# Making the convolution kernels inside the channel stage, and handing the last channel's rows over in SBUF

## The reference

```
x = x + mask * (causal_conv(x * mask, K) + D * x)   # K[h, l] = 2 Re sum_n Cs[h,n] exp(dtA[h,n] * l)
x = x + A1[id1] @ (B1[id1] @ x)                     # 8 adapters of rank 16
x = x + A2[id2] @ (B2[id2] @ x)                     # 64 adapters of rank 16
x = x + W[id3]^T x + bias[id3]                      # 32 matrices 64 x 64
```

## Time and profile before

| | |
|---|---|
| median of three runs | 784.39 us |
| the profiled execution | 783.29 us |
| its span, first to last instruction | 781.5 us |
| setup stage | 0 to 76 us |
| channel stage | 76 to 500 us |
| pair stage | 502 to 781.5 us |
| PE busy | 708.0 us (91%) |
| DVE busy | 624.3 us (80%) |
| ACT busy | 331.2 us (42%) |
| POOL busy | 393.9 us (50%) |
| granted clock of TensorE, mean | 0.989 |
| moved by DMA | 219.95 MB, mean 281 GB/s |

### The profile page before, as it was taken

The page is one execution under the profiler, slowest core; times in us unless marked ns, Lnnn a source line. Parts: engine busy times, 40 slices in busy tenths (PEclk is TensorE's granted clock), DMA queues, the critical chain, the costliest instruction groups (busy, mean ns, idle before and its releaser), DMA issues.

```text
span 781.5 us, 19175 instructions
## 1 busy us (share of the span) xinstructions
PE 708.0 (91%) x6688; PEld 541.4 (69%) x6688; DVE 624.3 (80%) x1124; ACT 331.2 (42%) x432; POOL 393.9 (50%) x682
## 2 busy tenths in 40 slices
PE   3044899999999999999999999589999999999997
PEld 2044677778887788887777777367777777777774
DVE  7995888887887778777877777378888888888885
ACT  2611112333133333222211122058777777777775
POOL 2420588888860000004767700177667766776672
PEclk9999999999999999999999999789999999999999
DMA  4007999999999999999999995579999999999974
GB/s 154 0 1 186 312 315 299 338 325 322 332 345 338 323 331 333 335 288 333 283 319 295 311 301 160 196 265 319 311 321 324 314 318 317 315 321 315 321 264 159
DMA packets 121319, 219.95 MB, mean 281 GB/s; under 512 B 19828, under 2 KB 79796, under 8 KB 121268
## 3 DMA queue, kind: packets, MB, share of 16 engines
q1 hardware_dynamic: 102692, 166.59, 66.3%
q10 hardware_dynamic: 9360, 33.56, 11.0%
q0 software_dynamic: 9216, 19.15, 7.7%
HBM read 146.35 MB, written 72.91 MB: 281 GB/s over the span
## 4 chain that ended last, share of the span: by engine, by line
PE 86%; DVE 3%; DMA 1%; ACT 1%; issue 0%; DVEq 0%; SPq 0%; ACTq 0%
PE ps L973 42%; PE ps L1261 11%; PE ps L1248 7%; PE ps L161 7%; PE ps L1294 6%; PE ps L1277 3%; PE ps L1276 3%; PE ps L1267 2%; PE ps L1034 1%; PE ps L1306 1%; PE ps L1018 1%; PE ps L1026 1%; DVE x1l L1235 1%; DMA xt<-x_rows 0%; DVE xTl L1216 0%; ACT xTh L1175 0%
## 5 line engine op out<-in xcount | busy, mean ns | idle before, releaser
L973 PE MATMUL ps<-toep,xTh 128*128 128x512 f16 (+3 forms) x1024 | 209.9, 300 | 0.0
L973 PE MATMUL ps<-toep,xTl 128*128 128x512 f16 (+3 forms) x512 | 147.0, 300 | 0.0
L783 POOL DMA_INDIRECT gnow<-g_rows,idx_g x64 | 58.8, 919 | 153.6 <-DMA g_rows<-g_out 127.4
L973 PEld LDWEIGHTS ps<-toep,xTh 128*128 128x128 f16 x1024 | 97.9, 98 | 51.1 <-issue 1.1
L1131 POOL DMA_INDIRECT asel<-a_rows,idx_a x64 | 72.2, 1129 | 77.3 <-PE ps L1277 76.2
L167 ACT ACTIVATE xS<-ps 128x256 f32<-128x256 f32 x64 | 24.4, 381 | 176.8 <-PE ps L161 176.8
L176 DVE TENSOR_TENSOR xTl<-ps,xTh 128x1024 f16<-128x1024 f32 x64 | 78.3, 1223 | 24.9 <-ACT xTh L168 24.6
L1126 POOL COPY bsel<-bt 128x256 f16 x256 | 92.7, 405 | 2.4 <-issue 1.7
L758 POOL DMA_INDIRECT wnow<-in_L_cond_weights,idx_w x64 | 62.1, 970 | 55.4 <-DVEq L920 38.4
L1216 DVE TENSOR_TENSOR xTl<-ps,xTh 128x1024 f16<-128x1024 f32 x64 | 78.3, 1224 | 12.3 <-ACT xTh L1175 9.0
L973 PE MATMUL ps<-diff,xTh 128*128 128x256 f16 x512 | 87.3, 273 | 0.0
(11 more groups left out here) (225 smaller groups left out, 1649.1 us busy)
## 6 DMA issues: line engine op xcount, KB each, us to landing
toep<-k_rows SPq DMA_DIRECT2D x64, 384.0 KB, 6.5
diff<-d_rows SPq DMA_DIRECT2D x64, 384.0 KB, 8.0
xt<-in_x SPq DMA_DIRECT2D x32, 512.0 KB, 6.3
x_rows<-xt ACTq DMA_DIRECT2D x32, 512.0 KB, 6.1
xt<-x_rows SPq DMA_DIRECT2D x32, 512.0 KB, 7.3
out_dram<-outt SPq DMA_DIRECT2D x32, 512.0 KB, 7.9
out_dram<-diff SPq DMA_DIRECT2D x32, 512.0 KB
toep<-x_rows SPq DMA_DIRECT2D x24, 512.0 KB
```

Of the source, the lines that this page charges most:

```text
L783: gp.indirect_dma_start(m.gnow[:, v, :], None, m.g_rows, bass.IndirectOffsetOnAxis(ap=m.idx_g[0:64, q:q + 1], axis=0)).then_inc(g_gathered ...
L973: last = PE.matmul(out, xs[x_part], rhs(part), start=start and k == 0, stop=stop and k == 2)
```

## The change

- K is made in eight chunks of eight channels. The setup stage makes chunk 0 only; chunks 1 to 7 are made in turns 0 to 6 of the channel stage, in pieces put into the lists of DVE, ACT, PE and SP at given channels u of a turn: the sines at u = 0 (ACT), combining at 1, the factors at 2 (both DVE), four products at 2 (PE), the first element at 3 (DVE), high and low parts at 4 (ACT, DVE), eight stores at 5 (SP, which then waits until they have landed), decays at 6 and 7 (ACT, sixteen small exponentials) and the turns of the chunk after at 6 and 7 (DVE).
- The sum's high part and the copy of the common part go from VectorE to ScalarE (`high_sum`, `copy_common`). `copy_common` of channel h-1 stands before the store of h-2 and waits for the convolution of h-1.
- The first seven channels of x are loaded in the setup stage. The rest of the setup (first adapters' turned A, bias, index rows) goes into the first turn of the channel stage (`finish_setup`).
- GpSimd waits for four gathers with one semaphore. Turns 5 and 6 are written out instead of a loop.
- For the first three pairs, channels 0 to 62 are loaded from DRAM as soon as these have landed, and the rows of channel 63 are copied from its SBUF tile; the DRAM copy of channel 63 is waited for only before the pairs from 3 on.

```diff
+E = 8
+CHUNKS = H // E
+KP = E // 2
+EARLY = 3
...
+def high_sum(nc, m, act, h, u):
+    act.wait_ge(m.xS_summed, h + 1)
+    nc.scalar.activation(m.xSh[:, u % 2, :, :], m.xS[:, u % 2, :, :], ACT.Copy).then_inc(m.xSh_ready, 1)
...
+def k_decay(nc, m, k, dst, s, ready):
+    for e in range(E):
+        nc.scalar.activation(dst[:, e, :], m.step[:, s, :], ACT.Exp, scale=m.par[:, 0, bass.ds(k * E + e, 1)]).then_inc(ready, 1)
...
+def k_products(nc, m, pe, k, bank):
+    pe.wait_ge(m.tables_ready, k + 1)
+    for q in range(KP):
+        last = nc.tensor.matmul(k_bank(m, bank)[:, q, :].rearrange("p (e c) -> p e c", e=2), m.u_all[:, 2 * q:2 * q + 2, :].rearrange("p e a -> p (e a)"),
+                                m.tv[:, q:E:KP, :], start=True, stop=True)
+    last.then_inc(m.k_done, 1)
...
+def store_k(m, sp, k):
+    sp.wait_ge(m.khl_ready, 2 * k + 2)
+    for e in range(2):
+        for n, rows in enumerate((m.k_rows, m.d_rows)):
+            for part in range(2):
+                dst = rows[bass.ds(k * E + e * KP, KP), part, 0:L].rearrange("q (a c) -> a q c", c=TC)
+                sp.dma_start(dst, m.khl[64 * e + 32 * n:64 * e + 32 * n + 32, part, :, :]).then_inc(m.k_stored, 16)
...
 (channel stage, SP)
+                            if make_k and u == XU - 3:
+                                store_k(m, sp, i + 1)
+                                sp.wait_ge(m.k_stored, 128 * (i + 2))
                             load_toeplitz(m, sp, h + 3, (u + 3) % U)
...
+                for p in range(EARLY):
+                    for b in range(2):
+                        sp.dma_start(x1_slot(m, p)[H * b:H * b + H - 1, :], m.x1_rows[2 * p + b, 0:H - 1, :]).then_inc(m.x1_parts[p], 16)
+                sp.wait_ge(low_ready, H)
+                sp.wait_ge(x1_ready, H)
+                for p in range(EARLY):
+                    sp.dma_start(x1_slot(m, p)[H - 1:P:H, :], x_slot(m, XU - 1)[2 * p:2 * p + 2, :]).then_inc(m.x1_parts[p], 16)
...
 (channel stage, ACT)
+                def copy_common(h, early):
+                    act.wait_ge(conv_done, h + 1)
+                    if not early:
+                        act.wait_ge(common_added, h)
+                    S.activation(m.common[:], conv_common, ACT.Copy).then_inc(common_copied, 1)
...
                             high_x(nc, m, u)
+                            high_sum(nc, m, act, h, u)
+                            copy_common(h - 1, first and u < 2)
                         if not (first and u < 2):
                             store_x1(h - 2, (u - 2) % XU)
+                        if make_k and u == 0:
+                            k_trig(nc, m, act, i + 1)
+                        if make_k and u == 4:
+                            act.wait_ge(m.k_stored, 128 * (i + 1))
+                            k_high(nc, m, act, i + 1, 3)
+                        if start_k and u == 6:
+                            act.wait_ge(m.tables_ready, i + 2)
+                            k_decay(nc, m, i + 2, m.dv, 0, m.decay_v_ready)
+                        if start_k and u == 7:
+                            k_decay(nc, m, i + 2, m.du, 1, m.decay_u_ready)
...
                 turns(act, body)
+                copy_common(H - 1, False)
                 store_x1(H - 2, XU - 2)
...
 (channel stage, DVE)
-                        dve.wait_ge(conv_done, h + 1)
-                        V.tensor_copy(m.common[:], conv_common).then_inc(common_added, 1)
-                        dve.wait_ge(common_added, 2 * h + 1)
+                        if make_k and u == 1:
+                            k_combine(nc, m, dve, i + 1)
+                        if make_k and u == 2:
+                            k_tables(nc, m, dve, i + 1)
+                        if make_k and u == 3:
+                            k_first(nc, m, dve, i + 1, 3)
+                        if make_k and u == 4:
+                            k_low(nc, m, dve, i + 1, 3)
+                        if start_k and u == 6:
+                            k_turns_u(nc, m, dve, i + 2)
+                        if start_k and u == 7:
+                            k_turns_v(nc, m, dve, i + 2)
+                        if first:
+                            finish_setup(u)
+                        dve.wait_ge(common_copied, h + 1)
```

More of the change, by code:

```diff
@@ L176, in low_x @@
     V.tensor_tensor(m.xTl[:, u % 2, :, :], m.turned, m.xTh[:, u % 2, :, :], ALU.subtract).then_inc(m.xTl_ready, 1)
[L177 to L183, removed]
+    dve.wait_ge(m.xS_summed, h + 1)
@@ new lines, in k_high, with k_low @@
+def k_high(nc, m, act, k, bank):
+    act.wait_ge(m.k0_added, k + 1)
+    for e in range(2):
+        rows = slice(64 * e, 64 * e + 64)
+        nc.scalar.activation(m.khl[rows, 0, :, :], k_bank(m, bank)[rows, :, e * TC:e * TC + TC], ACT.Copy).then_inc(m.k_high, 1)
+def k_low(nc, m, dve, k, bank):
+    dve.wait_ge(m.k_high, 2 * k + 2)
+    for e in range(2):
+        rows = slice(64 * e, 64 * e + 64)
+        nc.vector.tensor_tensor(m.khl[rows, 1, :, :], k_bank(m, bank)[rows, :, e * TC:e * TC + TC], m.khl[rows, 0, :, :],
+                                ALU.subtract).then_inc(m.khl_ready, 1)
@@ L317, in _ @@
+                sp.dma_start(m.biases[:], bias.rearrange("s o d -> s (o d)")).then_inc(m.bias_loaded, 16)
                 sp.wait_ge(const_made, 4)
-                sp.dma_start(m.k_rows[:, :, L:KPAD].rearrange("h s z -> (h s) z"), zeros[:]).then_inc(k_stored, 16)
+                sp.dma_start(m.k_rows[:, :, L:KPAD].rearrange("h s z -> (h s) z"), zeros[:]).then_inc(pad_stored, 16)
                 sp.dma_start(m.g_rows[GROW:GROW + R, :], ident[0:R, 0:R]).then_inc(m.g_stored, 16)
[L320 to L326, removed]
@@ L374, in _ @@
                              blocks(4).rearrange("p k t -> p t k"), ACT.Copy, scale=A_SCALE).then_inc(a_high, 1)
[L376 to L397, removed]
+                act.wait_ge(b_turned, 1)
+                S.activation(m.bt[:, 0:N1, 0, :, :], by_adapter(blocks(2)), ACT.Copy).then_inc(m.b0_high, 1)
+                k_high(nc, m, act, 0, 6)
+                high_sum(nc, m, act, 0, 0)
+                act.wait_ge(m.tables_ready, 1)
+                k_decay(nc, m, 1, m.dv, 0, m.decay_v_ready)
+                k_decay(nc, m, 1, m.du, 1, m.decay_u_ready)
+                act.wait_ge(m.decay_v_ready, 2 * E)
+                act.wait_ge(m.decay_u_ready, 2 * E)
+                act.wait_ge(m.b0_high, 1)
             @block.tensor
@@ L543, in _ @@
[L543 to L549 removed]
+                dve.wait_ge(m.par01_ready, 1)
@@ L684, in turns @@
         def turns(eng, body):
-            body(0, first=True)
+            body(0, first=True, make_k=True, start_k=True)
             with eng.Fori(1, GROUPED) as i:
-                body(i, group=True, next_group=True)
-            body(GROUPED, group=True)
-            with eng.Fori(GROUPED + 1, TURNS - 1) as i:
-                body(i)
+                body(i, group=True, next_group=True, make_k=True, start_k=True)
+            body(GROUPED, group=True, make_k=True, start_k=True)
+            for i in range(GROUPED + 1, TURNS - 1):
+                body(i, make_k=True, start_k=i < TURNS - 2)
             body(TURNS - 1, last=True)
@@ L698, in load_x, with body @@
                     sp.dma_start(x_slot(m, u), x[:, bass.ds(h, 1), :].rearrange("b o t -> b (o t)")).then_inc(m.x_loaded[u], 16)
-                def body(i, first=False, last=False, group=False, next_group=False):
-                    if first:
-                        for h in range(3, XU - 1):
-                            load_x(h, h)
+                def body(i, first=False, last=False, group=False, next_group=False, make_k=False, start_k=False):
                     for u in range(XU):
@@ L888, in selection_rows, with col, row_columns @@
+                pf, lf, rf, sf = (m.colf[:, n:n + 1] for n in range(4))
+                def col(n, rows=slice(0, P)):
+                    return cols[rows, n:n + 1]
+                pair = m.idf[:].rearrange("p n (q b) -> p n b q", b=2)
+                def row_columns():
                     step_of(V.tensor_scalar(col(3), lf, -1.0, 1.0, ALU.mult, ALU.add))
```

470 lines of the change are left out of this document (260 added, 210 removed).

## The result

The changed kernel took 796.71 us in the median of four runs (791.39 to 798.96) against 783.95 of the kernel before; the ratio is 1.0147, interval 1.0109 to 1.0186. The forecast was 778. The profiled execution has a span of 794.2 us against 781.5.

What follows compares the result with a forecast made beforehand. Setup, whatever delays TensorE's next channel (TensorE always busy, DMA 93%), and the hole before the pair stage count; 781.5-40.7+8.4+1.2+0.5+2.0+5.5+10+4+2.5 = 774.9 us span, so 778 us median, range 760 to 797.

Steps and rivals of the forecast that it cites:

- The setup: Before the channel stage: 256 instead of 2,048 elements a step, stage starting 39.5 us earlier; 40.7 less with channel 1's wait.
- K's products: TensorE, seven more chunks in the channel stage: 1.2 us each, 8.4 us in all, bounds 5.9 and 11.8.
- one full place: VectorE, channel 6 of the first turn: row numbers and K need 5.6 us against 3.6 of room, 2.0 us.
- I cost them at nothing: VectorE's pieces of K, 1.1 to 1.5 us, lie in some 1.65 us freed per channel by the moved copies.
- ScalarE's bursts: Sines and exponentials, 3.0 us each, 1.1 beyond the slack: 5.5 us in turns 0, 5 and 6; bounds 0 and 10.
- rival 3: ScalarE's table switches hold it about twice the load's length, five ungrouped ones 1.3 us more each: 784.5 us; chance 0.07.
- cover it: Grouped turns: a group's transposes or products on TensorE, 0.9 to 1.3 us behind the same channel, cover ScalarE's bursts.
- the late stores: Channel stores 5.2 us later delay loads of A in grouped turns: 10 us taken, bounds 0 and 19.4.
- mostly in the same microseconds in which TensorE is held up by A: Channel stage: K's stores on SyncE's queue, 20 us at full price, overlap the stalls for A, so 4 us taken.
- The argument for taking half: Late stores: a later TensorE leaves the DMAs less to carry, so part lands earlier; 10 us instead of 19.4.
- Rival 2: SyncE's queue bounds the grouped turns: late stores 19.4 and K's stores 20, 39.4 instead of 14; 803 us, chance 0.18.
- The hole: From last convolution to the pair stage's first transposes: 2.5 us longer, bounds 2 earlier and 5 later.

Runs made afterwards that it cites:

- Experiment 4: Changed kernel with ScalarE's store issued ahead of the sum's high part and common copy, and B and A loaded one channel earlier: 774.96 us, ratio 0.9861.
- experiment 2: Kernel before with one wait added: the store of channel h-2 is issued only when the convolution of h-1 is done; 797.93 us, ratio 1.0178.
- experiment 5: Changed kernel with K's eight stores of a turn issued from ScalarE's queue in channel 5 instead of SyncE's: 803.83 us, ratio 1.0255.

## Why the prediction was wrong

**The setup** was right: 39.5 us less forecast, 39.2 measured; the wait of 2.1 us at channel 1 went too.

**K's products** were over-sized, as the changed kernel's chain of waits shows (start, length, what):

```profile
184.57 1.34 PE ps L1149 x24
185.91 0.89 PE ps L311 x8
186.81 0.88 PE ps L190 x8
```

0.89 us a chunk, 6.2 in all against 8.4 forecast, near the lower bound of 5.9.

**VectorE** had one full place, as forecast. The transposes behind the index steps come 2.9 us late (2.0 forecast); TensorE's timeline in the changed kernel (start, length, engine, line, operation, idle before):

```profile
97.83 1.33 PE L190 MATMUL ps<-ident,xt 128*128 128x128 f32 x8 [2.89 <-DVE xSl L216]
```

But "I cost them at nothing" did not hold for its other pieces. In each of the four grouped turns TensorE waits, before it turns a group's B, for the low part of K that VectorE writes (us, times, longest):

```profile
PE ps L1116 <- DVE khl L336: 4.8, 4, 2.0
```

**ScalarE's bursts** had the right form. ScalarE's timeline in the third turn of the changed kernel:

```profile
222.90 1.28 ACT L265 ACT_TABLE_LOAD   x1 [0.28 <-issue]
224.20 0.42 ACT L265 ACTIVATE k_su<-k_tu 128x256 f32<-128x256 f32 x1
...
225.43 0.51 ACT L270 ACTIVATE k_tv<-k_tv,phase 128x256 f32<-128x256 f32 x1
```

3.0 us from the load to the last sine, as forecast, and the step behind the load starts at once, as in the earlier trace rows; rival 3 is out. From the transposes at 357.56 to the end at 502.47, 23 convolutions and 22 transpositions of 6.1 us in sum and two chunks are 141.0 us; it took 144.9. Turns 5 and 6 so cost 3.9 us; the forecast had 4.4 for the bursts and 0.8 for waits on the tables. The first turn cost more: from 37.12 to 97.83 us there are 50.9 us of work in 60.7, of which 2.9 are the index steps and 1.9 the first transposes and convolution (1.94 and 6.01 instead of 0.87 and 5.22). Of the other 5 us, 1.9 are K's products at 60.29 waiting for VectorE (line 949) and 1.4 the transposes and the convolution behind them, slow as behind every wait (1.71 and 5.81); the rest I did not part.

**The step that failed** is the price of the grouped turns: beyond the work in them the sum had 14 us, and 30.1 were measured. By the transposes that ended stalls (97.83, 169.61, 234.42, 298.44, 357.56) the grouped part took 71.8, 64.8, 64.0 and 59.1 us. The work is 33 channels of 6.1, eight groups of 3.08 and four chunks of 0.89, by stretches 62.8, 55.9, 55.9 and 55.0: 9.0, 8.9, 8.1 and 4.1 over. TensorE stood idle for 20.1 us of them. Nearly all the rest is work at the lower clock behind a wait: the transposes and the convolution that began at 97.83, 169.61, 234.42 and 298.44 took 8.6 us more than at the full clock, a cost that the forecast had for no stall.

Experiment 4, in which nothing waits for A, parts the 30.1. The grouped part of the changed kernel, then of experiment 4, by the columns of the windows above:

```profile
97.83:357.56 259.73, 239.59 (x2003) 188.19 (x2003) 181.48 (x299) 128.38 (x265) 125.45 (x128) 0.96 0.88 285
```

```profile
97.93:338.85 240.92, 234.82 (x2002) 185.88 (x2003) 179.47 (x299) 127.56 (x265) 125.44 (x128) 0.99 0.93 307
```

First, 11.3 us are left there over the same work, and the sum had nothing for them. It had said of ScalarE's bursts that in the grouped turns a group's transposes or products "cover it", and of VectorE's pieces "I cost them at nothing". TensorE's waits in the grouped part of experiment 4, behind the one for the index steps (us, times, longest), and the chain into one of the first kind:

```profile
PE ps L190 <- DVE xSl L216: 2.8, 4, 0.9
PE ps L311 <- DVE k_tv L299: 1.7, 1, 1.7
PE ps L1117 <- DVE khl L336: 1.5, 4, 0.4
```

```profile
275.19 1.28 ACT L265
...
278.15 0.95 ACT outt L893
...
282.42 1.06 PE ps L190 x8
```

The table load and the sines stand in the same channel as the reordering of A, and the high part of x comes behind both; the forecast had looked at each by itself. These waits are 6.0 of the 11.3; the lower clock behind them and behind the index steps is most of the rest.

Second, the late stores and K's stores, through A, cost 18.8 us (259.7 against 240.9) where the sum had 10 and 4. Neither price was far off by itself: the late stores cost 12.2 in experiment 2, and loading A early when the stores are first saves 2.9 (243.8 against 240.9), which is the most that K's stores can still cost there by way of A. Together they cost more than the sum of the two, and this is what failed in "mostly in the same microseconds in which TensorE is held up by A". The three long waits in the grouped part (4.6, 5.2 and 4.8 us, at 169.61, 234.42 and 298.44) all stand behind an A of channel 0, whose load has a late store and K's stores in front of it in one queue, one behind the other. The argument for taking half, that a waiting TensorE lets "part" land earlier, is borne out in part only. A itself landed no sooner, 11.2, 11.4, 12.1 and 9.7 us in the four chains and 9.4 in the median of experiment 2 against 9.6 before; the stores from two of their three tiles did in experiment 2 (4.3 and 4.8 instead of 6.0 and 5.9, medians). Why the shift of 5.2 reached A with 2.8 only was not settled. Rival 2, both at full price (39.4) and 803 us, had the right direction and the right queue, but its price was not reached.

**The hole** was mis-sized as well, 4.8 against 2.5 (and 1.8 more behind it, in the pair stage). The store of channel 62 landed in 2.6 us, sooner than the 3.5 assumed, but the copies needed more, by the changed kernel's chain of waits:

```profile
502.56 2.61 DMA x_rows<-x1l
507.89 7.13 DMA xt<-x1l
515.10 1.98 PE ps L1384 x8
```

The forecast had the first pair complete 6.1 us behind the landing of that store (T+4.3 and T+10.4). It was 9.9, of which the copies are 7.1, counted from their own first issue.

Summed over the forecast's 774.9, in us: the grouped part +16.1 (11.3 that stood at nothing, 4.8 for the stores); the hole with what follows it +4.1; the setup +0.3; K's products -2.2; turns 5 and 6 -1.3; the bias term, in no place of its own, -0.5. For the first turn the forecast had 3.1 of index steps and sines, 0.4 of a wait for tables, and what the kernel before already loses there: its stage takes 420.1 us for 390.4 of channels and 24.8 of groups, 4.9 over, of which the change was to save 1.2. That is 7.2 against 9.8, +2.6. The sum is 794.0; measured is 794.2.

## What to carry to other kernels

When work is inserted ahead of a DMA issue, price the issue, not the work. Follow the DMA to whoever waits for it, then to whatever that queue issues next, and compare the shift with the slack of the last link. Here the slack was 0.3 us at one line, the shift 5.2, and one swap of two lines was worth 19 us. What such a shift costs did not follow from the slack alone: alone it cost 12.2 us of a full price of 19.4, and with eight stores in front of the same load more than both apart. One run with nothing but the shift gives the price.

Work that is "covered" has to be covered in the place where it stands. Here ScalarE's burst of 3.0 us was to be covered by a group's products, but the reordering of A stands on ScalarE in the same channel; the grouped turns held 11 us at places where the forecast had nothing.

## What the runs showed that I had not expected

- Eight stores of 8 KB, 64 bytes a piece, took 5.5 us of ScalarE's queue in the third turn of experiment 5. On SyncE's they took 3.8 us in the first turn of the changed kernel and 5.0 in the third. The price is about the same; on SyncE it is paid by no computing engine.
- Copies of two rows of 4 KB from SBUF to SBUF took 5.6 to 7.7 us from the first issue until the pair stage could use them, behind or beside 1.5 MB of loads, longer than a whole pair (512 KB) took from DRAM in the kernel before, 3.7 us.
- A stall costs more than its own length. The granted clock was 0.95 to 0.98 in the turns with stalls and full behind them, and the transposes right behind a long one took 1.3 to 2.0 us instead of 0.87, the convolution 6.3 to 6.8 instead of 5.22: some 2 us for each. The mean clock of a whole execution does not show this: the kernel before took 784.15 us at 0.945 and 784.46 at 0.991.
